# Moving the weight fold from the norm stage into the feed-forward-up stage, with split loads and stores in the down stage

## The reference

```python
xn = layernorm(x)                                     # over the last axis
q = feature_map(xn @ Wq.T); k = feature_map(xn @ Wk.T); v = xn @ Wv.T   # 16 heads of 128
attn = tril((q k^T / sqrt(128)) ** 2)
o = attn v / (rowsum(attn) + 1e-5);  a = o @ Wo.T
hidden = silu(xn @ W1.T) * (xn @ W3.T)                # [2048, 8192]
hidden = fwht(hidden)                                 # Walsh-Hadamard over 8192, / sqrt(8192)
out = x + a + hidden @ W2.T
```

## Time and profile before

| | us |
|---|---|
| median of 2 runs (6177.3 and 6193.14) | 6185.22 |
| the profiled execution | 6188.32 |
| its span on the slowest core (core 1) | 6186.7 |
| spans of the eight cores | 6123.4 to 6186.7 |
| PE busy, share of the span | 4758.5, 77% |
| DVE busy | 1180.9, 19% |
| ACT busy | 1070.3, 17% |

### The profile page before, as it was taken

One profiled execution on the slowest core, in us unless ns is written; L12 is line 12 of the kernel. 1 busy time (PEld: TensorE's weight loads), 2 busy tenths in 40 slices (PEclk: granted clock), 3 DMA queues, 4 the chain that ended last, 5 costly groups with the idle time before them and its releaser, 6 DMA issues.

```text
span 6186.7 us, 68881 instructions; the slowest of 8 cores (6123.4 to 6186.7 us)
## 1 busy us (share of the span) xinstructions
PE 4758.5 (77%) x23090; PEld 2241.1 (36%) x23090; DVE 1180.9 (19%) x2744; ACT 1070.3 (17%) x1939; POOL 119.4 (2%) x220
## 2 busy tenths in 40 slices
PE   2334567667866775675779999999999989797978
PEld 0011243324322532342334444444444433343433
DVE  5664123213211321132110000000000000000000
ACT  0001215321522252234001111111111110000000
POOL 0000000000000000000000000000000000000000
PEclk9998886778677767776889999999999999898989
DMA  6673110121012101102542222222222226656575
GB/s 189 197 193 102 41 28 15 38 48 18 11 41 45 18 11 45 38 11 58 137 145 57 58 52 60 53 59 53 56 58 53 60 68 190 203 159 204 157 204 160
DMA packets 235864, 524.73 MB, mean 85 GB/s; under 512 B 18438, under 2 KB 108550, under 8 KB 223238
## 3 DMA queue, kind: packets, MB, share of 16 engines
q10 hardware_dynamic: 91392, 218.13, 11.8%
q0 software_dynamic: 46464, 117.45, 11.8%
q1 hardware_dynamic: 97670, 184.74, 8.9%
HBM read 528.65 MB, written 109.05 MB: 103 GB/s over the span
## 4 chain that ended last, share of the span: by engine, by line
PE 68%; DMA 10%; DVE 9%; ACT 5%; issue 4%; another core or an unknown queue 1%; SPq 1%; ACTq 1%; DVEq 1%; POOL 0%; POOLq 0%
PE ps_g L908 14%; PE ps_u L916 14%; PE ps_o L1035 14%; PE ps_y L474 6%; PE ps_y L596 4%; PE ps_ao L848 4%; PE ps_rb L644 4%; PE ps_oz L715 2%; DMA w2pp_scr<-foldst 2%; DVE foldst L263 2%; DMA wslab<-wk 2%; DMA wslab<-wq 2%; ACT attnS L650 2%; ACT ych L509 1%; DVE wlo L450 1%
## 5 line engine op out<-in xcount | busy, mean ns | idle before, releaser
L1035 PE MATMUL ps_o<-w2sl,u_sl 128*128 128x512 bf16 x4096 | 909.7, 386 | 176.5 <-DMA u_sl<-u_scr 137.8
L908 PE MATMUL ps_g<-xnT,w1sl 128*128 128x512 bf16 x4096 | 928.5, 380 | 15.5 <-DMA w3sl<-w 15.5
L916 PE MATMUL ps_u<-xnT,w3sl 128*128 128x512 bf16 x4096 | 925.8, 379 | 0.0
L1035 PEld LDWEIGHTS ps_o<-w2sl,u_sl 128*128 128x128 bf16 x4096 | 405.1, 99 | 681.1 <-issue 214.8
L908 PEld LDWEIGHTS ps_g<-xnT,w1sl 128*128 128x128 bf16 x4096 | 401.4, 98 | 501.1 <-issue 19.6
L916 PEld LDWEIGHTS ps_u<-xnT,w3sl 128*128 128x128 bf16 x4096 | 400.8, 98 | 483.3
L474 PE MATMUL ps_y<-xnT,wslab 128*128 128x512 bf16 x2048 | 544.9, 430 | 7.6 <-DMA wslab<-wk 7.2
L936 DVE TENSOR_TENSOR hidst<-silust,ps_u 128x512 bf16<-128x512 f32 x256 | 176.1, 688 | 1666.9 <-ACT silust L931 1666.9
L947 ACT ACTIVATE ust<-ps_uh 128x512 bf16<-128x512 f32 x256 | 152.9, 597 | 1489.6 <-PE ps_uh L942 1489.6
L644 PE MATMUL ps_rb<-ybq,ybk 128*128 128x512 bf16 x640 | 315.8, 543 | 71.7 <-ACT attnS L650 29.5
L514 PE MATMUL ps_rb<-ych,onedm_s 128*128 128x512 bf16 x128 | 59.2, 463 | 397.9 <-ACT ych L509 397.9
(11 more groups left out here) (92 smaller groups left out, 2400.6 us busy)
## 6 DMA issues: line engine op xcount, KB each, us to landing
w2sl<-w2pp_scr ACTq DMA_DIRECT2D x256, 512.0 KB, 4.1
w2pb<-w2p SPq DMA_DIRECT2D x32, 1024.0 KB, 7.8
w2pp_scr<-foldst ACTq DMA_DIRECT2D x128, 256.0 KB, 6.6
w1sl<-w POOLq DMA_DIRECT2D x64, 512.0 KB, 5.5
w3sl<-w POOLq DMA_DIRECT2D x64, 512.0 KB, 7.7
u_scr<-ust SPq DMA_DIRECT2D x256, 128.0 KB, 2.3
u_sl<-u_scr SPq DMA_DIRECT2D x32, 1024.0 KB, 15.0
w2pb<-w2p POOLq DMA_DIRECT2D x32, 512.0 KB, 8.0
```

What stands on the lines that cost most here:

```text
L908: em.op("tensor", lambda e, cb=cb, bb=bb, dc=dc, tc=tc: e.matmul(ps_g[cb][:], w1sl[bb][:, dc * 128:(dc + 1) * 128], xnT[:, dc * T + tc * 5 ...
L916: pv3 = em.op("tensor", lambda e, cb=cb, bb=bb, dc=dc, tc=tc: e.matmul(ps_u3[cb][:], w3sl[bb][:, dc * 128:(dc + 1) * 128], xnT[:, dc * T + ...
L1035: pv = em.op("tensor", lambda e, ttl=ttl, dd5=dd5, wb=wb, hb=hb, hq=hq: e.matmul(ps_o[ttl * 2 + dd5][:], u_sl[:, hb * 512 + ttl * 128: hb ...
```

## The change

The fold leaves the norm stage. It is done in the up stage, one job per block: all loads on SP into one f32 buffer (issued a block ahead), the cast to bf16 on DVE at chunk 0 of the block, the matmuls, evacuations and stores at chunk 2, after that chunk's matmuls and ahead of the epilogue of chunk 1. `wslab` and `vslab` are allocated for good, and the barrier after the norm stage no longer holds POOL back. To make room, the output projection loads x straight into `accst` and adds in place. In the down stage `u_sl` is loaded in two halves with tokens of their own: half A for the next chunk is issued when the second pass is through its 16th slab, half B after its last matmul. `outst` holds half a tile's columns and is stored after each pass.

```diff
+    wslab = [sb(f"wslab_{i}", [128, 2048], BF16) for i in range(2)]
+    vslab = sb("vslab", [128, 4096], BF16)
@@ norm stage: w2pb, w2pb32, foldst, ps_f, emit_w2pload, emit_fold_job taken out
-        for _fj in range(4):
-            emit_fold_job(j * 4 + _fj)
@@ after the norm stage
-    barrier()
+    sn_ln = snap()
+    for e_ in ("tensor", "vector", "scalar", "sync"):
+        em.waitsnap(e_, sn_ln)
@@ output projection
-    xres = [wsb(f"xres_{i}", [128, 2048], F32) for i in range(2)]
+            em.wait("sync", *gtok(f"accst{xb}"))
             em.wait("sync", *gtok(f"xres{xb}"))
             em.op("sync", lambda e, xb=xb, tt=tt: e.dma_start(
-                out=xres[xb][:], in_=x_d[tt * 128:(tt + 1) * 128, :]), s_xr[xb], 16)
+                out=accst[xb][:], in_=x_d[tt * 128:(tt + 1) * 128, :]), s_xr[xb], 16)
@@
                 dv = em.op("vector", lambda e, pb=pb, xb=xb, ddc=ddc: e.tensor_add(
                     accst[xb][:, ddc * 512:(ddc + 1) * 512], ps_ao[pb][:],
-                    xres[xb][:, ddc * 512:(ddc + 1) * 512]), s_dve)
+                    accst[xb][:, ddc * 512:(ddc + 1) * 512]), s_dve)
@@ up stage: two w2pb, one w2pb32, two foldst, two PSUM banks ps_f
+    def emit_w2pload(blk_i):
+        em.wait("sync", *gtok("w2pb32"))
+        em.op("sync", ... e.dma_start(
+            out=w2pb32[:], in_=w2p_d[blk_i * 128:(blk_i + 1) * 128, :]), s_w2p32, 16)
+    def emit_w2pcast(blk_i):
+        bb = blk_i % 2
+        em.wait("vector", s_w2p32, 0)
+        em.wait("vector", *gtok(f"w2pb{bb}"))
+        dv = em.op("vector", ... e.tensor_copy(w2pb[bb][:], w2pb32[:]), s_dve)
+    def emit_fold_job(blk_i):
+        for ddc in range(4):
+            pb = ddc % 2
+            em.wait("tensor", *gtok(f"w2pb{bb}_rdy"))
+            em.wait("tensor", *gtok(f"ps_f{pb}"))
+            pv = em.op("tensor", ... e.matmul(ps_f[pb][:], h64d[:],
+                w2pb[bb][:, ddc * 512:(ddc + 1) * 512], start=True, stop=True), s_pe)
+            em.wait("vector", s_pe, pv)
+            if ddc == 0:
+                em.wait("vector", *gtok(f"foldst{fs}"))
+            dv = em.op("vector", ... e.tensor_scalar_mul(
+                foldst[fs][:, ddc * 512:(ddc + 1) * 512], ps_f[pb][:], RSQ), s_dve)
+        em.wait("scalar", s_dve, dv_last)
+        for bit in range(2):
+            em.op("scalar", ... e.dma_start(
+                out=w2pp_view[2 * blk_i + bit],
+                in_=foldst[fs][bit * 64:(bit + 1) * 64, :]), s_fst[fs], 16)
@@
+    emit_w2pload(0)
     for st in range(NHB * NTC):
         blk_i, tc = divmod(st, NTC)
-        if tc == 0 and blk_i + 1 < NHB:
-            emit_wAload(blk_i + 1)
+        if tc == 0:
+            if blk_i + 1 < NHB:
+                emit_wAload(blk_i + 1)
+            emit_w2pcast(blk_i)
+            if blk_i + 1 < NHB:
+                emit_w2pload(blk_i + 1)
         emit_ffn_up(st)
+        if tc == 2:
+            emit_fold_job(blk_i)
         if st >= 1:
             emit_ffn_epi(st - 1)
@@ down stage
-    outst = [bsb(f"outst_{i}", [128, 2048], F32) for i in range(4)]
+    outst = [bsb(f"outst_{i}", [128, 1024], F32) for i in range(4)]
+    def emit_uload(tc, half):
+        em.wait("sync", *gtok("u_slA" if half == 0 else "u_slB"))
+        for part in range(4 * half, 4 * half + 4):
+            em.op("sync", ... u_sl part, s_usl if half == 0 else s_uslB, 16)
+    emit_uload(0, 0)
+    emit_uload(0, 1)
@@ in the slab loop, after a slab's matmuls
+                if ddh == 1 and qd == NQ // 2 - 1:
+                    tok["u_slA"] = (s_pe, pv)
+                    if tc + 1 < NTC:
+                        emit_uload(tc + 1, 0)
             if ddh == 1:
-                tok["u_sl"] = (s_pe, pv_fin)
+                tok["u_slB"] = (s_pe, pv_fin)
+                if tc + 1 < NTC:
+                    emit_uload(tc + 1, 1)
@@ after the two adds of each ttl, in both passes
+                em.wait("sync", s_dve, ttl_dv)
+                em.op("sync", lambda e, ttl=ttl, tt=tt, ddh=ddh: e.dma_start(
+                    out=out_d[tt * 128:(tt + 1) * 128, ddh * 1024:(ddh + 1) * 1024],
+                    in_=outst[ttl][:]), s_outB, 16)
@@ after both passes
-        em.wait("sync", s_dve, dv_last)
-        for ttl in range(4):
-            ... store of the whole tile, 1 MB
```

More of the change, by code:

```diff
@@ L211, in build_program @@
     tok_pstr = [(s_dve, dv), (s_dve, 0)]
[L213 to L270, removed]
-            em.op(q, lambda e, blk_i=blk_i, bit=bit, fs=fs: e.dma_start(
-                out=w2pp_view[2 * blk_i + bit],
-                in_=foldst[fs][bit * 64:(bit + 1) * 64, :]), s_fst[fs], 16)
-        tok[f"foldst{fs}"] = (s_fst[fs], 0)
@@ L276, in build_program @@
-    emit_w2pload(0)
-    emit_w2pload(1)
-    emit_w2pload(2)
     def emit_xload(j):
@@ L400, in build_program @@
     invk_tmp = gsb("invk_tmp", [128, 16], F32)
-    wslab = [gsb(f"wslab_{i}", [128, 2048], BF16) for i in range(2)]
-    vslab = gsb("vslab", [128, 4096], BF16)
     ych = [gsb(f"ych_{i}", [128, 512], BF16) for i in range(2)]
@@ L884, in build_program @@
     ust = [fsb(f"ust_{i}", [128, 512], BF16) for i in range(2)]
+    w2pb = [fsb(f"w2pb_{i}", [128, 2048], BF16) for i in range(2)]
+    w2pb32 = fsb("w2pb32", [128, 2048], F32)
+    foldst = [fsb(f"foldst_{i}", [128, 2048], BF16) for i in range(2)]
     ps_g = [fps(f"ps_g_{i}", [128, 512]) for i in range(2)]
@@ L987, in build_program @@
     acc_view = acc_scr.rearrange("(tcg ttl p) d -> tcg p ttl d", ttl=4, p=128)
-    for tc in range(NTC):
-        em.wait("sync", *gtok("u_sl"))
-        for part in range(8):
+    def emit_uload(tc, half):
+        em.wait("sync", *gtok("u_slA" if half == 0 else "u_slB"))
+        for part in range(4 * half, 4 * half + 4):
             em.op("sync", lambda e, tc=tc, part=part: e.dma_start(
@@ L994, in build_program @@
                 in_=u_view[:, part * 8:(part + 1) * 8, tc * 512:(tc + 1) * 512]),
-                s_usl if part < 4 else s_uslB, 16)
+                s_usl if half == 0 else s_uslB, 16)
+    emit_uload(0, 0)
+    emit_uload(0, 1)
+    for tc in range(NTC):
         dv_last = None
@@ L1057, in build_program @@
                     tok[f"ps_o{k}"] = (s_dve, dv)
+                    ttl_dv = dv
                     dv_last = dv
-            tok["acc_sl"] = (s_dve, dv_last)
-        em.wait("sync", s_dve, dv_last)
-        for ttl in range(4):
-            tt = tc * 4 + ttl
-            em.op("sync", lambda e, ttl=ttl, tt=tt: e.dma_start(
-                out=out_d[tt * 128:(tt + 1) * 128, :], in_=outst[ttl][:]), s_outB, 16)
-        for ttl in range(4):
-            tok[f"outst{ttl}"] = (s_outB, 0)
+                tt = tc * 4 + ttl
+                em.wait("sync", s_dve, ttl_dv)
+                em.op("sync", lambda e, ttl=ttl, tt=tt, ddh=ddh: e.dma_start(
+                    out=out_d[tt * 128:(tt + 1) * 128, ddh * 1024:(ddh + 1) * 1024],
+                    in_=outst[ttl][:]), s_outB, 16)
+                tok[f"outst{ttl}"] = (s_outB, 0)
+            tok["acc_sl"] = (s_dve, dv_last)
     em.wait("sync", s_outB, 0)
```

34 lines of the change are left out of this document (29 added, 5 removed).

## The result

The changed kernel is slower: 1.044 times the kernel before, 95% interval 1.038 to 1.051. Many executions of both kernels were disturbed (the cores of one die at a lower clock); all times from here on are of executions free of this or nearly so, and where a run's profile had one such die, its rows are of a core on the other.

The account below looks back on a forecast made before the run. PE's matmuls were taken to bound the kernel, so fold work on PE's queue costs its full length. 6188.3 - 357 - 6 + 2 + 595 - 64 + 6 - 7 = 6357, forecast as 6355 us; 8 in 10: 6250 to 6430.

Parts of the forecast that it names:

- Norm stage: Start: without the 64 fold jobs a tile takes 10.25 us, -357; the first wk slab is ready in SBUF, -6.
- Attention and output projection: Middle stages: nothing moves, loading x into accst costs 0; one more 1 MB load at the next stage's start, +2.
- The fold's chain: Up stage: evacuations, DMA issues, silu and multiply delay the h128 matmul by 6.8 us per block, 64 blocks.
- The clock: Up stage: PE's empty gap lowers its clock, 12 slow matmuls cost 2.5 us per block, bounds 0 and 3.0.
- What hides the cast and the load: Up stage: w2p's cast falls in DVE idle time, its load is issued 28 us ahead: 0; without that cover, 79.
- Down stage: Last stage: shorter chunk-boundary gaps net of slab stalls, -64; half-size stores colliding with acc_sl loads, +6; shorter end, -7.
- The slab stalls: Last stage: half A's load beside dense matmuls delays w2sl slabs, 6 us per boundary, bounds 3 and 15.
- Contention eats part 4: Rival, last stage: slabs stall through both u halves and evacuations wait for stores; -64 becomes 0, 6420 us; chance 0.10.
- The fold is hidden: Rival, up stage: the chain runs under chunk 2's matmuls, only the fold's matmuls cost, 55 us; 5817 us; chance 0.08.
- The break-even of 6.7 us per block: Up stage: fold cost per block at which it cancels all other savings, 426 us together.

Follow-up runs that it names:

- gap filled: Changed kernel with 16 more matmuls, into a PSUM bank nobody reads, behind the fold's four in each block: 6317 to 6331 us, 1.021 times the kernel before.
- the run without the shared count: Changed kernel with one semaphore per output buffer instead of one shared by all four: 6360 to 6365 us, 1.025 times the kernel before.

## Why the prediction was wrong

The direction was right, the size was not: 6355 was forecast with 6430 at most, and the kernel takes 6452 to 6456. The steps in their order:

- **Norm stage, -357 and -6.** Right: -358 on the slowest cores. Over all cores the first projection matmul moved from 536 to 554 us to 193 to 195, -351 on average. The tile takes 182.62 - 172.37 = 10.25 us, as worked out. The first reduce came at 21.0 instead of 16.5, since x's first load took about 12 us beside the others, not 7 to 8, and the `wslab` wait went as forecast.
- **Attention and output projection, 0, and +2 for the load.** The load was +3 (18.55 us of waiting instead of 15.5). The stretch between is 34 us longer on the slowest core against the slowest core, but that compares two cores: over all eight it was 2679 to 2713 us before and 2701 to 2736 after, means 2698 and 2720. So some +20 us were not in the working. Kernels with the same instructions in this part had means of 2687 (gap filled) to 2724, those with the norm stage of before 2699 and 2702. What makes the difference was not tested, and it stays open.
- **The fold's chain, 6.8 us per block.** Right: 6.94.
- **The clock, 2.5 us per block.** 2.1 by the difference of 9.0 and 6.94 and by the blocks in which the filling held the level. The term was 25 us too large in all, within its bounds.
- **What hides the cast and the load.** Right: no row of the up stage waits for them after the start.
- **Down stage, -64, +6 and -7.** This is the step that failed: +28. The boundary gap was put at 9.5 us, as the later of the evacuations (6.66) and the first slab; it was 33.7 to 35.1. The inner boundary was left at 6.66; at three of the four it was 16.4 to 17.8. The working priced the new output stores as transfers that contend, +1.5 us each time, and never asked what waits for them. They put a wait on DVE in every pass, behind which the evacuations queue and then PE. The diff showed it: the `if ddh == 0 and dd5 == 0` in front of the wait became `if dd5 == 0`, and the stores moved into the loop over `ttl`. With the shared count gone, the same working holds: 7.9 to 8.6 us for 9.5, 6.7 to 7.1 for the inner boundary.
- **The slab stalls, 6 us per chunk with bounds 3 and 15.** In the run without the shared count the stalls in mid-pass, where half A is loaded, are 7.7 us in all, 2.6 per chunk and just under the lower bound. But the stalls behind the three chunk boundaries, which the working took to be the same before and after, are 18.7 us where the kernel before had 9.7. Together that is 16.7 us where 18 were taken: the sum came out by two errors that cancel. The +6 for the inner boundaries was 5.2 us of slab waits behind them.
- **The rivals.** *Contention eats part 4* gave 6420 with 0.10 and was the nearest in size. Its sentence "the evacuations wait for stores" names the event, but as an effect of traffic, not of a semaphore's count. The stores took 2.6 to 10.4 us to land in the changed kernel, 3.7 in the median; with a semaphore per buffer they took longer, 6.9 in the median and up to 18.6, and DVE waited for none of them. *The fold is hidden* did not come true as the change stands; with the fold spread over the chunks it did, 56 us for its 55.

With the shared count gone the kernel takes 6360 us, 5 from the forecast of 6355. So the shared count accounts for 92 of the 97 us by which 6452 exceeds the forecast. That the rest is so small is luck: the clock was put 25 us too high, and the 20 us of the first part were not seen. The break-even of 6.7 us per block was too high for the kernel as it stands: its other parts save 358 - 34 - 28 = 296 us, 4.6 per block. With 9.0 it lost, and with 2.5 and the shared count still in, 6034 beat 6177.
